# Attention scores and row maxima in two 64-row tiles of TensorE, in a two-layer transformer kernel

## The reference

```python
xn = layernorm(x)
x = x + L0_attn(xn) + L0_ffn(xn)   # 32 query heads of 16, 8 key heads; softmax(q k / 4) v; then Wo
                                   # ffn: gelu(xn @ W1 + b1) @ W2 + b2, 2048 wide
xn = layernorm(x)
x = x + L1_attn(xn) + L1_ffn(xn)   # causal, biases, rotary embedding on q and k; scale 1/16
                                   # ffn: (silu(x1) * x2) @ w3 + b3, 512 wide
```

## Time and profile before

| what | value |
|---|---|
| median of the runs | 596.59 us |
| profiled execution, its time / its span | 596.43 / 594.7 us |
| busy share TensorE, VectorE, ScalarE, GpSimd | 95%, 77%, 59%, 39% |
| granted clock of TensorE over the span | 0.997 |
| first score step at, first of layer 2, first of the last unit | 41.7, 372.8, 573.6 us |

### The profile page before, as it was taken

How to read it: one execution, slowest core, us unless ns; L and a number is a source line. 1 busy time by engine, 2 the same in 40 slices (tenths; PEclk the granted TensorE clock), 3 DMA queues, 4 the chain that set the end, 5 groups by cost and what they waited for, 6 DMA issues and landing times.

```text
span 594.7 us, 10503 instructions
## 1 busy us (share of the span) xinstructions
PE 563.2 (95%) x3216; PEld 435.0 (73%) x3216; DVE 456.5 (77%) x1232; ACT 348.0 (59%) x598; POOL 232.6 (39%) x345
## 2 busy tenths in 40 slices
PE   3979999999999999999999999899899999998997
PEld 3967777777777878777787787667677778766754
DVE  6487987765666687577899678898998989789673
ACT  3667756664564676376677276357645564565451
POOL 6231334713304521313223115264745485364242
PEclk9999999999999999999999999999999999999999
DMA  6993452453223244315433323336443443434101
GB/s 200 130 317 103 120 142 69 113 157 107 79 82 108 80 124 136 90 40 174 126 128 99 113 78 101 90 107 143 134 117 89 104 130 109 125 108 133 29 6 68
DMA packets 30535, 67.02 MB, mean 113 GB/s; under 512 B 4880, under 2 KB 18192, under 8 KB 28560
## 3 DMA queue, kind: packets, MB, share of 16 engines
q1 hardware_dynamic: 21840, 38.04, 24.5%
q0 software_dynamic: 8640, 28.32, 15.9%
HBM read 50.87 MB, written 13.63 MB: 108 GB/s over the span
## 4 chain that ended last, share of the span: by engine, by line
PE 79%; DVE 8%; issue 5%; DMA 3%; POOL 2%; ACT 2%; DVEq 0%; POOLq 0%; ACTq 0%
PE banks L766 53%; PE banks L826 8%; PE banks L874 8%; PE banks L852 7%; DMA q_sb<-max_t 2%; DVE banks L1156 2%; PE banks L786 1%; PE banks L855 1%; POOL probs L708 1%; DVE neg_max L1156 1%; DVE o_tok L1177 1%; DVE x_res L1200 1%; PE banks L835 1%; DVE bn L1054 1%; DVE hid L1221 1%
## 5 line engine op out<-in xcount | busy, mean ns | idle before, releaser
L988 ACT ACTIVATE probs<-banks 128x512 f32<-128x512 f32 (+1 forms) x256 | 138.0, 545 | 187.5 <-PE banks L852 149.2
L766 PE MATMUL banks<-xnT,w_up 128*128 128x512 f32 x576 | 153.8, 400 | 0.2
L1161 DVE TENSOR_REDUCE neg_max<-banks 128x2 f32<-128x512 f32 x128 | 87.4, 688 | 79.3 <-PE banks L826 77.9
L766 PE MATMUL banks<-w_down,hid 128*128 128x512 f32 x480 | 127.4, 399 | 0.0
L766 PEld LDWEIGHTS banks<-xnT,w_up 128*128 128x128 f32 x576 | 102.1, 190 | 30.6 <-issue 12.9
L826 PEld LDWEIGHTS banks<-k_sb,q_sb 96*128 96x128 f32 x512 | 92.5, 191 | 23.6 <-issue 5.5
L1156 DVE CUSTOM_DVE_ANT_0 banks<-banks,mask_qk 128x128 f32<-128x128 f32 (+1 forms) x256 | 86.3, 375 | 25.5 <-PE banks L826 24.9
L826 PE MATMUL banks<-k_sb,q_sb 96*128 96x256 f32 (+1 forms) x512 | 100.0, 277 | 5.4 <-issue 3.2
L766 PEld LDWEIGHTS banks<-w_down,hid 128*128 128x128 f32 x480 | 85.2, 188 | 25.7 <-DVE max_t L1169 5.9
L708 POOL TENSOR_SCALAR_AFFINE_SELECT probs<-probs 128x256 f32<-128x256 f32 x128 | 59.5, 465 | 75.9 <-ACT probs L988 69.3
L852 PE MATMUL banks<-q_sb,k_sb 97*128 97x512 f32 x192 | 78.8, 410 | 8.4 <-DMA q_sb<-max_t 7.0
(11 more groups left out here) (79 smaller groups left out, 655.3 us busy)
## 6 DMA issues: line engine op xcount, KB each, us to landing
q_sb<-q_parts SPq DMA_DIRECT2D x60, 256.0 KB, 4.8
raw<-in_up POOLq DMA_DIRECT2D x48, 256.0 KB, 3.4
raw<-in_down POOLq DMA_DIRECT2D x40, 256.0 KB, 3.1
q_parts<-stage SPq DMA_DIRECT2D x30, 256.0 KB, 2.5
raw<-in_attn POOLq DMA_DIRECT2D x20, 256.0 KB, 3.6
k_parts<-stage SPq DMA_DIRECT2D x14, 256.0 KB, 2.5
k_sb<-k_parts SPq DMA_DIRECT2D x14, 256.0 KB, 4.1
out<-x_res SPq DMA_DIRECT2D x8, 256.0 KB, 2.1
```

The source lines that it names most:

```text
L766: mm = nc.tensor.matmul(out_ap, lhs(a), rhs(b_), start=first and j == 0, stop=stop and j == 2, **kw)
L988: nc.scalar.activation(probs[:, i, 0:w], banks[:, ST_BANKS[k % 2], 0:w], ACT.Exp, scale=SCALES[n // B]).then_inc(exp_done, 1)
L1161: nc.vector.tensor_reduce(neg_max[:, s, 2 * g:2 * g + 2, t], banks[:, bank_of[x], :].rearrange("p (r t) -> p r t", r=2)[:, :, 0:w], AX.X, ...
```

## The change

Scores and maxima use 48 rows a head, not 96: parts q (hi, lo, hi) against k (hi, hi, lo), so three products. With the row of maxima that is 49. Two key heads lie side by side, one in partitions 0 to 48 and one in 64 to 112, and their matmuls are issued one after the other, as two tiles of 64 rows of TensorE's array. A step of `st` fills both score banks, a step of `m` two work banks; a unit has 4 steps of each, in the even slots. Values stand directly behind such a stretch. The gate and what follows it move to the next slot that has a score step. Loads of q become four DMAs a unit, the row of maxima two, loads of k two. The zero rows and what filled them are gone.

```diff
 UNITS = 2 * LU
-ROWS = 96
-MROW = 96
+HALF = 64
+ROWS = 48
+MROW = 48
+STEPS = 4
+STEP = -1
...
+Q_PARTS = (0, 1, 0)
+K_PARTS = (0, 0, 1)
...
-COST = {"up": 681, "down": 681, "wo": 693, "qkv": 363, "xn": 440, "v": 220, "st": 233, "m": 235, "mt": 110, "pv": 995}
+COST = {"up": 681, "down": 681, "wo": 693, "qkv": 363, "xn": 440, "v": 220, "st": 340, "m": 340, "mt": 110, "pv": 995}
...
     if x[0] == "up" and x[1] == 1:
         c = x[2]
         if x[3] == 0:
-            return [(0, ("gate", c))]
-        return [(0, ("hidden", 1, c)), (2, ("hidden_hi", 1, c)), (3, ("hidden_lo", 1, c))]
+            return [(STEP, ("gate", c))]
+        return [(STEP, ("hidden", 1, c)), (3, ("hidden_hi", 1, c)), (4, ("hidden_lo", 1, c))]
...
             for d, y in followers(x):
+                if d == STEP:
+                    d = [k for k in range(1, 4) if g + k >= len(slots) or any(z[0] == "st" for z in slots[g + k])][0]
...
-    o += [parts(("up", 0, 0, 0)) + [("load_q", 2), ("fill", 0)], parts(("up", 0, 1, 0))]
-    ms = spread([[("m", 0, i)] for i in range(8)], parts(("qkv", 1, 2)), [1] * 8)
-    later = parts(("qkv", 1, 0))
-    ms += spread([[("m", 1, i)] for i in range(4)], later, [1] * 4)
-    ms[1].append(("fill", 1))
-    ms[4].append(("fill", 2))
-    ms[7].append(("mrow", 0))
-    ms[8] += [("mt", 0), ("load_bias",)]
-    ms[9] += split(0, "up", 2, 3)
-    ms[10] += split(0, "down", 0, 1)
+    o += [parts(("up", 0, 0, 0)) + [("load_q", 2)], parts(("up", 0, 1, 0))]
+    ms = spread([[("m", 0, j)] if j < 4 else [] for j in range(5)], parts(("qkv", 1, 2)), [1] * 5)
+    ms += spread([[("m", 1, 0)], [], [("m", 1, 1)], []], parts(("qkv", 1, 0)), [1] * 4)
+    ms[4].append(("mrow", 0))
+    ms[5] += [("mt", 0), ("load_bias",)]
+    ms[6] += split(0, "up", 2, 3)
+    ms[7] += split(0, "down", 0, 1)
...
-    slots = [[("st", u, i)] for i in range(8)]
+    slots = [[] for i in range(8)]
     for i in range(8):
-        if i < 4 and u + 1 < UNITS:
-            slots[i].append(("m", u + 1, i + 4))
-        if i >= 4 and u + 2 < UNITS:
-            slots[i].append(("m", u + 2, i - 4))
+        j = i // 2
+        if i % 2 == 0:
+            slots[i].append(("st", u, j))
+        if i in (0, 2) and u + 1 < UNITS:
+            slots[i].append(("m", u + 1, j + 2))
+        if i in (4, 6) and u + 2 < UNITS:
+            slots[i].append(("m", u + 2, j - 2))
...
-        slots[1].append(("pv", u - 1, 1))
-        slots[2].append(("norm", u - 1, 0))
-        slots[3] += [("norm", u - 1, 1), ("norm", u - 1, 2)]
-        slots[4].append(("norm", u - 1, 3))
-        slots[5].append(("ctx", u - 1))
-    slots[5].append(("pv", u, 0))
+        slots[0 if u < LU else 2].append(("pv", u - 1, 1))
+        k = 1 if u < LU else 3
+        slots[k].append(("norm", u - 1, 0))
+        slots[k + 1] += [("norm", u - 1, 1), ("norm", u - 1, 2)]
+        slots[k + 2].append(("norm", u - 1, 3))
+        slots[k + 3].append(("ctx", u - 1))
+    slots[4 if u < LU else 6].append(("pv", u, 0))
...
-            k = [k for k in recent if k not in taken][0]
+            uses = [x + (a,) for a in range(2)] if x[0] == "m" else [x]
+            before[x] = []
+            for y in uses:
+                k = [k for k in recent if k not in taken][0]
+                recent.remove(k)
+                recent.append(k)
+                if k in user:
+                    before[x].append(user[k])
+                bank[y], user[k] = k, y
+                taken.add(k)
+            bank[x] = [bank[y] for y in uses] if x[0] == "m" else bank[x]
...
-                        sp_.wait_ge(st_filled, st_index(u - RING, 7) + 1)
-                    for e in range(2):
-                        sp_.dma_start(q_sb[32 * e:32 * e + 32, u % RING, :, :].rearrange("p g t -> p (g t)").bitcast(F32),
-                                      qscr[n, s]).then_inc(q_loaded[u % RING], 16)
+                        sp_.wait_ge(st_filled, st_index(u - RING, STEPS - 1) + 1)
+                    for a in range(2):
+                        src = qscr0[n, s, a] if n < B else qscr1[n - B, s, :, a, :]
+                        to = q_sb[HALF * a:HALF * a + ROWS, u % RING, :, :].rearrange("p c t -> p (c t)").bitcast(F32)
+                        sp_.dma_start(to[0:2 * HD], src).then_inc(q_loaded[u % RING], 16)
+                        sp_.dma_start(to[2 * HD:], src[0:HD]).then_inc(q_loaded[u % RING], 16)
...
-                    g = slice(4 * f * T, (4 * f + 4) * T)
-                    sp_.dma_start(k_sb[0:4 * HD, 4 * f:4 * f + 4, :].rearrange("p g t -> p (g t)").bitcast(F32),
-                                  kscr[n].rearrange("q d x -> (q d) x")[:, g]).then_inc(k_loaded[f], 16)
+                        sp_.wait_ge(st_filled, st_index(S * (n - 1) + 2 * f + 1, STEPS - 1) + 1)
+                    g = slice(2 * f * T, (2 * f + 2) * T)
+                    for a in range(2):
+                        src = kscr0[n, a] if n < B else kscr1[n - B, :, a, :]
+                        to = k_sb[HALF * a:HALF * a + ROWS, 2 * f:2 * f + 2, :].rearrange("p c t -> p (c t)").bitcast(F32)
+                        sp_.dma_start(to, src[:, g]).then_inc(k_loaded[f], 16)
...
-                    sp_.dma_start(q_sb[MROW:MROW + 1, u % RING, :, :].rearrange("o h t -> o (h t)").bitcast(F32),
-                                  max_t[:, u % 2, :].bitcast(F32)).then_inc(m_loaded[u % RING], 16)
+                        sp_.wait_ge(st_filled, st_index(u - RING, STEPS - 1) + 1)
+                    for a in range(2):
+                        row = HALF * a + MROW
+                        sp_.dma_start(q_sb[row:row + 1, u % RING, :, :].rearrange("o c t -> o (c t)").bitcast(F32),
+                                      max_t[8 * a:8 * a + 8, u % 2, :].bitcast(F32)).then_inc(m_loaded[u % RING], 16)
...
                     w = T if n < B or t == 1 else P
                     for r in range(2):
-                        mm = nc.tensor.matmul(banks[:, k, r * T:r * T + w],
-                                              q_sb[0:ROWS, u % RING, 2 * g + r, t * P:t * P + P], k_sb[0:ROWS, 4 * f + g, 0:w],
-                                              start=r == 0, stop=r == 1, skip_group_check=True)
+                        for a in range(2):
+                            rows = slice(HALF * a, HALF * a + ROWS)
+                            mm = nc.tensor.matmul(banks[:, ks[a], r * T:r * T + w],
+                                                  q_sb[rows, u % RING, 2 * c + r, t * P:t * P + P], k_sb[rows, 2 * f + c, 0:w],
+                                                  start=r == 0, stop=r == 1, skip_group_check=True)
                     mm.then_inc(wk_filled, 1)
...
-                    t, g = divmod(i, 4)
-                    k = st_index(u, i)
-                    bank_k = ST_BANKS[k % 2]
-                    if k >= 2:
-                        pe.wait_ge(exp_done, k - 1)
-                    if k == 0:
-                        pe.wait_ge(made, ALL_MADE)
-                    if i == 0:
-                        pe.wait_ge(m_loaded[u % RING], 16 * (u // RING + 1))
-                    keys = k_sb[0:MROW + 1, 4 * f + g, t * P:t * P + P]
-                    bank = banks[:, bank_k, :].rearrange("p (r t) -> p r t", r=2)
-                    if n < B or t == 0:
-                        mm = nc.tensor.matmul(bank, keys, q_sb[0:MROW + 1, u % RING, 2 * g:2 * g + 2, :], start=True, stop=True)
-                    else:
-                        later = banks[:, bank_k, 0:2 * P].rearrange("p (r t) -> p r t", r=2)
-                        mm = nc.tensor.matmul(later, keys, q_sb[0:MROW + 1, u % RING, 2 * g:2 * g + 2, P:], start=True, stop=True)
+                    t, c = divmod(j, 2)
+                    if st_index(u, j):
+                        pe.wait_ge(exp_done, 2 * st_index(u, j))
+                    if j == 0:
+                        pe.wait_ge(m_loaded[u % RING], 32 * (u // RING + 1))
+                    q0 = 0 if n < B or t == 0 else P
+                    for a in range(2):
+                        rows = slice(HALF * a, HALF * a + MROW + 1)
+                        mm = nc.tensor.matmul(banks[:, ST_BANKS[a], 0:2 * (T - q0)].rearrange("p (r t) -> p r t", r=2),
+                                              k_sb[rows, 2 * f + c, t * P:t * P + P],
+                                              q_sb[rows, u % RING, 2 * c:2 * c + 2, q0:], start=True, stop=True)
                     mm.then_inc(st_filled, 1)
...
-                    t = i // 4
-                    k = st_index(u, i)
-                    act.wait_ge(st_filled, k + 1)
+                    t = j // 2
+                    act.wait_ge(st_filled, st_index(u, j) + 1)
                     if u:
                         act.wait_ge(pv_done, 2 * (u - 1) + t + 1)
                     w = 2 * P if n >= B and t == 1 else 512
-                    nc.scalar.activation(probs[:, i, 0:w], banks[:, ST_BANKS[k % 2], 0:w], ACT.Exp,
```

(14 more changed lines are left out.)

193 lines of the change are left out of this document (98 added, 95 removed).

## The result

The changed kernel takes **601.49 us** (median of 19 runs, 598.53 to 607.6), the kernel before 595.13 us (19 runs beside them). Ratio **1.0097, 95% interval 1.0068 to 1.0127**. Forecast were 582.5 us and a range of 560 to 600: size and sign were wrong. The profiled execution took 599.63 us, its span 597.9 us.

The account below looks back on a forecast made before the run. TensorE was taken as the bound (busy 95%), VectorE in some units of layer 2. TensorE -16.8, vector-bound units +2.5, banks +3.5, row of maxima -2 and end -1 sum to -13.8 us: 582.5 us, range 560 to 600.

Parts of the forecast that it names:

- Stretch, switches and values: TensorE: tiled stretches -7.5 us (large) and +3.3 (small), values sharing the stretch's way out -12.6; together -16.8 us.
- values' 12.6: TensorE: values directly behind a tiled stretch share its way out in 63 places, 0.20 us each, 12.6 us gained.
- Rivals 1 to 4: Tiled stretches: serial loads, 611 us (0.09); weights wait for matmul, 610 (0.04); tiles serial, 637 (0.03); cheap switches, 561 (0.15).
- +2.5: Vector-bound units of layer 2 cannot use TensorE's saving, so half of layer 2's 5 us comes back.
- SyncE ... I take nothing, with 2 us either way.: SyncE's queue: more issues for q and max rows weighed against fewer bytes and an earlier slot; zero, 2 us either way.
- late queries as a sign of failure: Layer 2: the prediction fails if q lands late there, or if a switch to row tiles has an unseen cost.
- Banks, +3.5 for nine fills: Maxima steps take two work banks that VectorE empties in turn; some nine fills wait 0.4 us each, +3.5 us.
- Row of maxima (-2): A unit's last maxima come three slots before its transpose, not two; two TensorE waits for neg_max should go, -2 us.
- End (-1): At the very end values no longer wait 0.95 us for the last mask, as six w_down matmuls stand between.
- a "nothing" of mine: Score steps wait for both exponentials of the step before on ScalarE, but two slots lie between steps: no cost.
- rival 5: Layer 2 gives it back: 64 stretches each wait 0.2 us for VectorE's second bank, 13 us, 595 us; chance 0.15.

Follow-up runs that it names:

- e2: Changed kernel with values, norms and ctx put back into the slots of the kernel before: ratio 1.0197 to the kernel before.
- e11: Kernel before with loads ahead of stores, rotation sum one slot later, statistics in unit 5, layer 2's maxima without causal mask: 593.13 us, ratio 0.9941.
- e10: Changed kernel with loads ahead of stores, rotation sum one slot later, statistics in unit 5, layer 2's maxima without causal mask: 579.11 us, ratio 0.9694.
- e1: Changed kernel with SyncE's loads of queries and keys ahead of the stores: ratio 0.9945 to the kernel before.
- e16: Kernel before with only the stores of layer 1 cut into four transfers in place of two: ratio 1.0086.
- e9: Changed kernel with loads ahead of stores, rotation sum one slot later, fourth sequence's statistics moved from unit 1 to 5: ratio 0.9861 to the kernel before.
- e6: Kernel before with SyncE's loads of queries and keys ahead of the stores: ratio 0.9965.
- e14: Kernel before with loads ahead of stores, rotation sum one slot later, statistics in unit 5, masks kept: ratio 1.0020.

## Why the prediction was wrong

**TensorE's terms: right.** Stretch, switches and values were forecast at 16.8 us of work, given as 11 and 5 by layer (0.8 is in neither). e2 gives 10.3 for the values' 12.6. e11 less e10 gives 10.3 and 8.7 of busy time; of the 8.7 some 1.8 are e11's clock (0.991 over 198.6 us, where e10 has 1.00), so about 7. Rivals 1 to 4 are out: the rows of 201 us have pairs side by side, loads hidden in the stretch and exposed at its ends. That the whole sum, -13.8, meets the -14.0 of the pair e10 and e11 is luck: the sum also holds +2.5 and +3.5 for VectorE and banks, -2 and -1 for maxima and end, which this pair, without masks, doesn't test.

**The step that failed: "SyncE ... I take nothing, with 2 us either way."** I counted three loads growing to six in layer 2, and not that a store of layer 1 grows from two issues to four and stands ahead of the loads. The change to the code showed both. The queue's way from store to last load grew by 3.1 us, and there was no slack: before, TensorE already waited 0.56, 0.38 and 0.24 us at 109, 130 and 281 us, in the same places. In layer 2, where I had looked and named late queries as a sign of failure, the term held: the last of the six issues landed at 378.85 us, before at 380.81. Measured: 7.1 us in layer 1 (e1; clock included), and from the other side 6.6 us in layer 1 for the stores alone in the old kernel (e16, whose profiled execution was its slowest; its median is 5.9 us above before).

**Banks, +3.5 for nine fills: too small in one place.** One fill alone, at 70 us, cost 3.82 us and the clock behind it; e9, against e1, recovers 5.6 us in unit 1. I had added row durations along the order as if VectorE began each reduce at once; there it was 4 us behind, with tiny steps of 1.2 and 1.7 us in that queue, each held until a step of GpSimd ended. No run moved GpSimd's steps alone.

**The clock had no term.** Layer 2 of the changed kernel does the matmuls of e10's. TensorE's busy time there is 185.4 us at a clock of 0.97, in e10 181.3 at 1.00 (e9: 187.9 at 0.97). So 4 to 7 us of TensorE's busy time in layer 2 is what running at 1.2 GHz adds. Of the 4.9 us by which layer 2 missed its forecast the clock can thus be up to 4.1; how much of that other waits would have taken up, no run tells. Before, the clock in the two layers was 0.99 and 1.00, so I had no price for it.

**Row of maxima (-2): wrong sign.** The wait of L873 for neg_max is 3.6 us, not zero; the row itself is one issue longer. **End (-1): nothing came of it.** At 577.89 scores wait 2.20 us for two exponentials that stand behind casts on ScalarE (a "nothing" of mine). That the last stage is 1.6 us longer is the clock behind this wait: in e1 the wait is the same 2.20 us, the clock stayed up, and the stage took 21.1 us as before; the old kernel lost the clock there in e6 and e16 and took 22.7.

**Layer 2: rival 5, in part.** It had 13 us for second banks and 595 us. The waits for banks are there (4.2 us at 421 and 479 us), with rows of maxima and the clock. With VectorE lighter by 17 us the saving returns (e10, e11: 3.2 us), so it is VectorE's load that held it back. That layer 2 is 0.7 us longer than the old one at equal edits (e9, e14) is within what the clock moves it; whether the load acts by bursts of four reduces, later rows or the clock, stays open.

In numbers, forecast against measured by stage: layer 1 -9 and +0.2, layer 2 -3 and +1.9, the end -1 and +1.6. So layer 1 is the largest part of the miss, 9.2 us; e9, with the edits for the queue and for unit 1, takes 12.0 us off it (331.3 to 319.3), a little more than was missed, where the same edits took 0.8 us off the old kernel's (e14).

## What to carry to other kernels

Count every issue that a new layout adds on each DMA queue, stores too, and walk the queue in order up to the load that someone waits for; where TensorE already waited a few tenths of a microsecond for the load, half a microsecond an issue decided. A saving on the busiest engine is only had where the others keep up: a layout that needs two banks, two issues and two exponentials at once wants its loads, statistics and copies re-placed, and then it pays (here 14 us). A wait on TensorE can cost twice, since the clock fell behind five of the nine over 2 us here. Before a small step on VectorE is taken as free, look at what GpSimd does at that time.
